# Moving the decay multiply of two batch groups in a clipped recurrence from VectorE to ScalarE

## The chip, the cores and the metric

The kernel runs on one core of a Trainium2 chip. A core has engines with queues of their own: PE (TensorE: matmuls and transposes, with weight loads as PEld), DVE (VectorE), ACT (ScalarE), POOL (GpSimd) and SP (SyncE, which here only issues DMAs). Each engine takes its own instructions in order, and they wait for each other through semaphores. The metric is the device time of one execution in microseconds; less is better.

## What is computed

Four layers run one after the other on x of 32 batches, 128 tokens and 512 channels: a recurrent layer, two attention layers, and a second recurrent layer. The change touches the two recurrent layers. Cut to what matters, the reference computes this in each of them:

```python
xr, gate = split(x @ W_in.T)            # 1024 channels each; xr: bias, convolution over 4 tokens, silu
xn = layernorm(xr)
Bm, Cm, dt = split(xn @ W_xproj.T, 3)   # 16 states each
Ad = 1.0 + tanh(dt @ W_dt.T + b_dt) * 0.01 * -tanh(A_log)
Bd = Bm * minimum(norm(xn), 1.0)
def step(h, inputs):                    # h: 16 states x 1024 channels for each batch
    ad, bd, xt, ct = inputs
    h = clip(h * ad[:, :, None] + bd[:, :, None] * xt[:, None, :], -10.0, 10.0)
    return h, einsum('bd,bdh->bh', ct, h)
_, ys = scan(step, h0, (Ad, Bd, xn, Cm))
out = x + (ys + D * xn) * silu(gate) @ W_out.T
```

So each token multiplies the state by a decay for each batch and state, adds an outer product, clips at 10, and reads the state out.

## The kernel before, in words

A recurrent layer has two phases, with a barrier between them. The first, `project_phase` (names `l0a`, `l3a`), does everything that doesn't depend on the state. The second, `recurrence_phase` (names `l0r`, `l3r`), is the one that is changed. It runs four engines in step, under an order that is written out by hand for each of them.

**The state.** 32 batches are 4 groups (`GJ`, index j) of 8. 8 batches with 16 states each fill the 128 partitions, so the state of one group is a tile of 128 x 1024 in f32. `g[:, t, j, :]` holds it for the last 4 tokens (`TS`, index t). 128 tokens are 32 blocks (`NBLK`, index k) of 4, so a block has 16 VectorE operations. They are numbered n = 4t + j here, and "op 10" is the one with t = 2 and j = 2. The two layers have 512 each.

**The scaled state.** The state is kept divided by the running product of its decays, `prod`. Then no step has to multiply by a decay: the input term is divided by `prod` ahead of time (`feed`), the coefficients that read the state out are multiplied by it, and the bounds of the clip become plus and minus 10 / `prod`, different for each partition and token. A setup on VectorE (lines 1165 to 1184) makes them; POOL copies those of one block into `cf` (`bounds`, line 925). One custom VectorE instruction does a step (line 1196): it adds the new term from PSUM to the state of the token before and clips the sum between two scalars of one value per partition, read from `cf`.

**TensorE, for each block.** Eight slots, s = 2t + p. Each begins with a `spread` (line 999): four matmuls that write the outer products of ops n and n + 1 (n = 2s) into two of three PSUM tiles `pv`, which are used in turn. Since a tile is free only when VectorE has read it, `spread` waits for the op n - 2 (semaphore `gup`). Behind the `spread` each slot has one piece of other work (`after`, line 1054), in this order: a run of 8 matmuls of the output projection (`mix` run 1 for block k - 2), `read_out` of token 3 of block k - 1, `mix` run 2 for k - 2, `read_out` of token 0, `turns` (transposes of the gated output of k - 1, in two halves), `read_out` of token 1, `mix` run 0 for k - 1, `read_out` of token 2. `mix` run 0 waits for both halves of `zh` (semaphore `z_hi`, line 1044).

**ScalarE, for each block** (body at line 1119): `keep_y` copies the read-out from PSUM, `keep_out` the projected output; `high(k, m)` copies half m of the transposed output to `zt` (which frees the PSUM bank for the other half) and then, rounded, to `zh`. In the first block it first makes the rounded part `woh` of the 8 output weight tiles (lines 1123 to 1125).

**POOL, for each block** (body at line 957): `bounds`, `weigh` (the weights of the next block's `spread`, from `crow`, which SP loads), `gating` of the last half block, `readers` (the coefficients of the next block's `read_out`), `residual`, `low` twice, `gating`. In the first block it waits for all eight `woh` tiles in between (lines 967 to 971), and makes the remainders `wol`.

**SP.** It loads the weight tiles through a buffer of two, `wst`: tile c waits for the remainder of tile c - 2. Only behind the eighth comes the load of `crow` for block 2.

**VectorE, for each op** (line 1186): it waits until its own earlier op is done (`gup`) and until its outer product is in PSUM (`bmm`). At the first op of a token it also waits until the old state of that place has been read out (`ymm`).

Of the kernel before, what the change touches and what calls it, by code (L numbers as in the profile page):

```python
# [6 lines left out]
ALU = mybir.AluOpType  # L7
ACT = mybir.ActivationFunctionType
# [6 lines left out]
KD, KI = DM // P, DI // P  # L15
# [5 lines left out]
CLIP = 10.0  # L21
GJ = 4
GB = B // GJ
TS = 4
# [3 lines left out]
PAIR = 2  # L28
ROOM = 2 * GB + 1
ROUND = 6  # L30
HEAD = 4


class Phase:
# [34 lines left out]
def at_least(eng, sem, value):  # L69

    if not (isinstance(value, int) and value <= 0):
        eng.wait_ge(sem, value)


def hold(eng):

    eng.nop(nofuse=True)
# [695 lines left out]
def recurrence_phase(nc, tag, x_in, x_out, w, cst, dram, proj, stat, wsum, wbias, coef, sent):  # L773

    with Phase(nc, tag) as ph:
        g = ph.sb("g", [P, TS, GJ, DI])
# [6 lines left out]
        cf = ph.sb("cf", [P, 2, 3, TS, GJ])  # L783
# [9 lines left out]
        wst = ph.sb("wst", [P, 2, DM])  # L793
        woh = ph.sb("woh", [P, KI, DM], F32R)
        wol = ph.sb("wol", [P, KI, DM], F32R)
        pv = [ph.ps(f"pv{k}", DI) for k in range(3)]
# [9 lines left out]
        zero = g[:, 1, 2, 0:S]  # L806
# [13 lines left out]
        z_mm, z_ev, z_hi, z_lo, o_mm, o_ev, res, w_hi, w_lo = (ph.sem(n) for n in (  # L820
            "z_mm", "z_ev", "z_hi", "z_lo", "o_mm", "o_ev", "res", "w_hi", "w_lo"))
        zeroed, last_sum, last_z, last_res = (ph.sem(n) for n in ("zeroed", "last_sum", "last_z", "last_res"))
        block = ph.block()
        n_pairs = NBLK // 2
        JW = TS * GB
# [82 lines left out]
        def _(pool):  # L908
# [5 lines left out]
            pool.memset(cd[:, :, :, :, :], 0.0).then_inc(zeroed, 1)  # L914
            pool.wait_ge(zeroed, 1)
            pool.wait_ge(same_ld, 32)
            pool.wait_ge(step, 8 + 3 + GJ + 1 + 3)

            def weigh(k, q, uses):
                pool.wait_ge(cr_ld[q], 32 * uses)  # L920
# [168 lines left out]
        def _(act):  # L1089
# [9 lines left out]
            act.wait_ge(feed_turned, 1)  # L1099
            act.activation(feed_h.rearrange("s j i -> s (j i)"), pf, ACT.Copy).then_inc(feed_high, 1)  # L1100

            def keep_y(k, m):
                act.wait_ge(ymm, TS * k + PAIR * (m + 1))
                at_least(act, z_mm, PAIR * (k - 1) + m + 1)
                act.activation(y[:, m, :], py[:, :], ACT.Copy).then_inc(yev, 1)  # L1105

            def high(k, m):
                act.wait_ge(z_mm, PAIR * k + m + 1)
                at_least(act, o_mm, k)
                act.activation(zt[:, :, m, :], pzo[:, :].rearrange("p (e i) -> p e i", i=TS * GB), ACT.Copy).then_inc(z_ev, 1)  # L1110
                act.wait_ge(z_ev, PAIR * k + m + 1)
                act.activation(zh[:, :, m, :], zt[:, :, m, :], ACT.Copy).then_inc(z_hi, 1)

            def keep_out(k):
                act.wait_ge(o_mm, k + 1)
                at_least(act, res, k)
                act.activation(mixed[:, :], pzo[:, :], ACT.Copy).then_inc(o_ev, 1)

            def body(i, first, last):
                for q in range(2):  # L1120
                    k = 2 * i + q
                    if first and q == 0:
                        for c in range(KI):
                            act.wait_ge(w_ld[c % 2], 16 * (c // 2 + 1))
                            act.activation(woh[:, c, :], wst[:, c % 2, :], ACT.Copy).then_inc(w_hi, 1)
                    if not (first and q == 0):
                        keep_y(k - 1, 1)
                    if not first:
                        keep_out(k - 2)
                    if not (first and q == 0):  # L1130
                        high(k - 1, 0)
                        high(k - 1, 1)
                    keep_y(k, 0)

            blocks(act, n_pairs, body)
            for m in range(PAIR):
# [8 lines left out]
        def _(dve):  # L1145
            count = [0]

            def chain(ins):

                count[0] += 1  # L1150
                ins.then_inc(step, 1)
                dve.wait_ge(step, count[0])
# [15 lines left out]
            chain(dve.tensor_scalar(acol[:, 1:2], acol[:, 0:1], -0.01, None, ALU.mult))  # L1168
            chain(dve.tensor_scalar(decay, decay, acol[:, 1:2], 1.0, ALU.mult, ALU.add))
            for j in range(GJ):  # L1170
                chain(dve.tensor_tensor_scan(prod[:, j, :], decay[:, j, :], zero, 1.0, ALU.mult, ALU.add))
            chain(dve.reciprocal(inv, prod))
            out = [coef[:, c, :, :].rearrange("p s j -> p j s") for c in range(3)]
            turn = [pt[c].rearrange("p (j s) -> p j s", j=GJ) for c in range(2)]
# [1 line left out]
            dve.tensor_tensor(feed, turn[0], inv, ALU.mult).then_inc(fed, 1)  # L1176
            chain(dve.tensor_tensor(out[2], turn[1], prod, ALU.mult))
            chain(dve.tensor_scalar(out[0], inv, CLIP, None, ALU.mult))
            dve.wait_ge(feed_high, 1)
            dve.tensor_tensor(feed_l.rearrange("s j i -> s (j i)"), pf, feed_h.bitcast(F32).rearrange("s j i -> s (j i)"),  # L1180
                              ALU.subtract).then_inc(feed_low, 1)
# [4 lines left out]
            def body(k):  # L1186
                dve.wait_ge(cfc, k.count(1, 1))
                for t in range(TS):
                    for j in range(GJ):
                        n = GJ * t + j  # L1190
                        if j == 0:
                            at_least(dve, ymm, k.count(TS, t - TS + 1))
                        dve.wait_ge(gup, k.count(GJ * TS, n + 1))
                        dve.wait_ge(bmm, k.count(GJ * TS, n + 1))
                        hold(dve)
                        dve._custom_dve(bass.dve_ops.TENSOR_ADD_SAT, out=g[:, t, j, :],  # L1196
                                        in0=g[:, (t - 1) % TS, j, :], in1=pv[(k.off + t + j) % 3][:, :],
                                        s0=cf[:, k.parity(), 0, t, j:j + 1], s1=cf[:, k.parity(), 1, t, j:j + 1]).then_inc(gup, 1)

            rounds(dve, body)  # L1200
            dve.wait_ge(ymm, TS * NBLK)
# [1112 lines left out]
```

## Time and profile before

| what | us |
|---|---|
| median of 3 runs (3762.84 to 3764.57) | 3763.84 |
| the profiled execution's own time | 3766.1 |
| its span, first to last instruction | 3764.3 |
| first VectorE step of layer 0 | 525.81 |
| first VectorE step of layer 3 | 3100.15 |
| VectorE busy with the steps, layer 0 and layer 3 | 641.9 and 641.8 |

The profiled execution is 2.3 us above the median, and 1.8 us of its time lie outside its span. The differences that are worked out below come from its trace and are put on the median. Over the whole span PE is busy 91%, DVE 79%, ACT 36% and POOL 50%; but these are averages over phases with different limits. The views that matter are the timeline of a recurrent block, the idle time ahead of the groups of the recurrence, and the timeline of the first two blocks.

### The profile page before, as it was taken

The page shows a single profiled execution, that of the slowest core. Times are in us where ns is not written, and L with a number is a line of the kernel's source. Part 1 is how long each engine was busy: PE and PEld are TensorE (multiplying, and loading weights), DVE is VectorE, ACT ScalarE, POOL GpSimd, SP SyncE. Part 2 cuts the span into 40 slices and gives each one's busy share as a digit, 9 for nine tenths or more (in the row PEclk, how much of TensorE's full clock was granted, in tenths as well). Part 3 has the DMA queues.
Part 4 walks back from the last instruction along what each step waited for, and adds up shares of the span by engine and source line. Part 5 has one row for each costly group of instructions (what it writes and reads, how often), then busy time and mean ns, then how long its engine had stood idle before and what let it go on. Part 6 is the DMA issues. An engine that isn't in the chain of part 4 may idle for free. (4 is left out here: it accounts for less than half of the span.)

```text
span 3764.3 us, 62060 instructions
## 1 busy us (share of the span) xinstructions
PE 3412.0 (91%) x22068; PEld 2260.9 (60%) x22068; DVE 2965.0 (79%) x3172; ACT 1355.2 (36%) x2078; POOL 1868.6 (50%) x1384
## 2 busy tenths in 40 slices
PE   7999839999996899999999999997999948999998
PEld 6777614444443667777777777775777733444444
DVE  4777769999996777777778777763576769999998
ACT  3555512221222553444444444432455522122121
POOL 2555645655563024444454444433355655556554
PEclk9999959999998899999999999998999968999999
DMA  4566765565554224222322222224466675555553
GB/s 128 217 259 257 271 239 203 203 219 214 200 215 142 80 72 138 85 82 78 111 96 87 80 83 85 74 63 133 162 259 237 257 294 196 217 201 210 216 206 136
DMA packets 288573, 631.00 MB, mean 168 GB/s; under 512 B 33472, under 2 KB 35904, under 8 KB 288224
## 3 DMA queue, kind: packets, MB, share of 16 engines
q1 hardware_dynamic: 281200, 615.49, 46.6%
q10 hardware_dynamic: 7104, 11.81, 0.9%
q8 instruction: 183, 3.00, 0.3%
q14 instruction: 86, 0.70, 0.1%
HBM read 390.75 MB, written 241.70 MB: 168 GB/s over the span
## 5 line engine op out<-in xcount | busy, mean ns | idle before, releaser
L1196 DVE CUSTOM_DVE_ANT_0 l0r_g<-l0r_g,l0r_pv,l0r_cf 128x1024 f32<-128x1024 f32 x512 | 641.9, 1336 | 20.6 <-PE l0r_pv L1005 19.0
L1196 DVE CUSTOM_DVE_ANT_0 l3r_g<-l3r_g,l3r_pv,l3r_cf 128x1024 f32<-128x1024 f32 x512 | 641.8, 1337 | 17.8 <-PE l3r_pv L1005 16.2
L137 PE MATMUL l1h_ps_p<-l1h_xh,l1c_wh 128*128 128x512 f32 x768 | 323.3, 421 | 5.6 <-issue 3.3
L139 PE MATMUL l1h_ps_p<-l1h_xl,l1c_wh 128*128 128x512 f32 x768 | 306.3, 399 | 0.0
L138 PE MATMUL l1h_ps_p<-l1h_xh,l1c_wl 128*128 128x512 f32 x768 | 304.9, 397 | 0.0
L2182 POOL TENSOR_TENSOR l1h_st<-l1h_veps 128x1 f32<-128x1 f32 x64 | 35.4, 554 | 530.5 <-DVE l1h_veps L2040 530.5
L1794 ACT ACTIVATE l1h_pt<-l1h_ps_t 128x512 f32<-128x512 f32 x256 | 151.4, 591 | 330.7 <-PE l1h_ps_t L1667 330.7
L1020 PE MATMUL l0r_py<-l0r_g,l0r_cd 128*32 128x512 f32 x2048 | 253.1, 613 | 1.3 <-ACT l0r_y L1105 1.3
L1020 PE MATMUL l3r_py<-l3r_g,l3r_cd 128*32 128x512 f32 x2048 | 252.0, 611 | 0.8 <-ACT l3r_y L1105 0.8
L2080 DVE TENSOR_TENSOR l1h_e<-l1h_e,l1h_mx 128x1024 f32<-128x1024 f32 x128 | 207.2, 1619 | 4.4
L2099 DVE TENSOR_TENSOR l1h_vt<-l1h_ps_p,l1c_dc 128x512 f32<-128x512 f32 x64 | 44.3, 691 | 194.6 <-PE l1h_ps_p L139 194.6
L1005 PE MATMUL l0r_pv<-l0r_x,l0r_wv 32*128 32x512 f32 x1024 | 132.3, 503 | 50.6 <-DVE l0r_g L1196 29.7
L1787 ACT ACTIVATE l1h_e<-l1h_e 128x1024 f32<-128x1024 f32 x128 | 134.9, 1054 | 118.8 <-DVE l1h_e L2023 117.5
L1005 PEld LDWEIGHTS l0r_pv<-l0r_x,l0r_wv 32*128 32x128 f32 x1024 | 53.5, 185 | 206.3 <-issue 137.0
L1005 PE MATMUL l3r_pv<-l3r_x,l3r_wv 32*128 32x512 f32 x1024 | 131.4, 499 | 50.5 <-DVE l3r_g L1196 29.4
L1005 PEld LDWEIGHTS l3r_pv<-l3r_x,l3r_wv 32*128 32x128 f32 x1024 | 53.2, 184 | 205.8 <-issue 136.8
L627 DVE SCALAR_TENSOR_TENSOR l3a_pacc<-l3a_pad,l3a_wconv,l3a_pacc 128x512 f32<-128x512 f32 x192 | 144.8, 754 | 34.6 <-ACT l3a_pacc L485 30.1
L627 DVE SCALAR_TENSOR_TENSOR l0a_pacc<-l0a_pad,l0a_wconv,l0a_pacc 128x512 f32<-128x512 f32 x192 | 144.8, 754 | 34.1 <-ACT l0a_pacc L485 29.5
L2207 POOL TENSOR_TENSOR l1h_vl<-l1h_vt,l1h_vh 128x512 fp32r<-128x512 f32 x64 | 123.7, 1933 | 92.2 <-ACT l1h_vh L1825 92.2
L1667 PE MATMUL l1h_ps_t<-l1h_ident,l1h_e 128*128 128x128 f32 x1024 | 161.8, 281 | 6.4 <-ACT l1h_pt L1794 5.6
L139 PEld LDWEIGHTS l1h_ps_p<-l1h_xl,l1c_wh 128*128 128x128 f32 x768 | 145.9, 190 | 36.2
L137 PEld LDWEIGHTS l1h_ps_p<-l1h_xh,l1c_wh 128*128 128x128 f32 x768 | 146.4, 191 | 33.6 <-issue 4.3
(400 smaller groups left out, 8965.1 us busy)
## 6 DMA issues: line engine op xcount, KB each, us to landing
l0r_x<-xhl_s SPq DMA_DIRECT2D x128, 512.0 KB, 5.9
l3r_x<-xhl_s SPq DMA_DIRECT2D x128, 512.0 KB, 5.7
xhl_s<-l0a_xo SPq DMA_DIRECT2D x116, 512.0 KB, 4.6
xhl_s<-l3a_xo SPq DMA_DIRECT2D x116, 512.0 KB, 4.6
gate_s<-l0a_gate SPq DMA_DIRECT2D x64, 256.0 KB, 3.0
l0r_dx<-dx_s SPq DMA_DIRECT2D x32, 512.0 KB, 7.7
l0r_gate<-gate_s SPq DMA_DIRECT2D x32, 512.0 KB, 8.6
l0r_crow<-feed_s SPq DMA_DIRECT2D x64, 256.0 KB
```

The costliest lines, as they stand in the source:

```text
L137: pe.matmul(out, wh, xh, start=first, stop=False)
L138: pe.matmul(out, wl, xh, start=False, stop=False)
L139: return pe.matmul(out, wh, xl, start=False, stop=last)
L627: dve.scalar_tensor_tensor(out=a, in0=pad[:, it % 2, :, c:c + S], scalar=wconv[:, it, c:c + 1], in1=a, op0=ALU.mult, op1=ALU.add).then_inc ...
L1005: last = pe.matmul(pv[(k.off + t + 2 * p + a) % 3][:, h * HALF:(h + 1) * HALF], wv[r, k.parity(), 2 * t + p, :], x[r, k.parity(), t, p, :] ...
L1020: last = pe.matmul(py[j * JW:(j + 1) * JW, :], cd[:, k.parity(), t, j, at:at + JW], g[:, t, j, h * HALF:(h + 1) * HALF], start=t % 2 == 0 ...
L1196: dve._custom_dve(bass.dve_ops.TENSOR_ADD_SAT, out=g[:, t, j, :], in0=g[:, (t - 1) % TS, j, :], in1=pv[(k.off + t + j) % 3][:, :], s0=cf[: ...
L1667: last = pe.transpose(ps_t[:, h * S:(h + 1) * S], e[:, k.mod(2), u // 2, h, u % 2, :], ident[:, :])
L1787: act.activation(e[:, k.mod(2), half, :, :, :], e[:, k.mod(2), half, :, :, :], ACT.Exp).then_inc(exp_ok, 1)
L1794: act.activation(pt[:, u % 2, :, :], ps_t[:, :].rearrange("p (h s) -> p h s", h=HG), ACT.Copy).then_inc(pt_ok, 1)
L2080: dve.tensor_tensor(block, block, total.unsqueeze(3).to_broadcast([P, HG, 2, S]), ALU.mult).then_inc(en_ok, 1)
L2207: pool.tensor_tensor(vl[:, n.mod(2), :, :], vt[:, n.parity(), :, b * S:(b + 1) * S], vh[:, n.mod(2), :, :].bitcast(F32), ALU.subtract).the ...
```

## The change

Groups j = 0 and j = 2 (`ACTED`) keep the state unscaled. For them `prod` is 1, `cf` holds the decay in place of the upper bound, and a step is two instructions: ScalarE multiplies the state of the token before by the decay (`age`), into the place of the new one, and VectorE adds the PSUM term to it and clips, with the constants 10 and -10 in place of two values per partition. Groups 1 and 3 stay as they are. A semaphore `aged` tells VectorE that the multiply is done.

ScalarE's list for a block is rewritten around the multiplies. The two copies of `high` are separate functions now, `keep_z` (to `zt`) and `high` (to `zh`). The eight weight copies of the first block are cut in two: four at the end of block 0, four in block 1. The code of TensorE and SP is not changed, nor is POOL's, but for the count of setup steps it waits for. `HEAD` wasn't used.

```diff
-HEAD = 4
+ACTED = (0, 2)
...
+            def high_weights(lo, hi):
+                for c in range(lo, hi):
+                    act.wait_ge(w_ld[c % 2], 16 * (c // 2 + 1))
+                    act.activation(woh[:, c, :], wst[:, c % 2, :], ACT.Copy).then_inc(w_hi, 1)
+
...
-            def high(k, m):
+            def keep_z(k, m):
                 act.wait_ge(z_mm, PAIR * k + m + 1)
                 at_least(act, o_mm, k)
                 act.activation(zt[:, :, m, :], pzo[:, :].rearrange("p (e i) -> p e i", i=TS * GB), ACT.Copy).then_inc(z_ev, 1)
+
+            def high(k, m):
                 act.wait_ge(z_ev, PAIR * k + m + 1)
                 act.activation(zh[:, :, m, :], zt[:, :, m, :], ACT.Copy).then_inc(z_hi, 1)
+
+            def age(k, q, t):
+                for j in ACTED:
+                    if t == j == 0:
+                        act.wait_ge(cfc, k + 1)
+                    if j == ACTED[0]:
+                        at_least(act, ymm, TS * (k - 1) + t + 1)
+                    act.wait_ge(gup, GJ * TS * k + GJ * t + j + 1)
+                    act.activation(g[:, t, j, :], g[:, (t - 1) % TS, j, :], ACT.Copy, scale=cf[:, q, 0, t, j:j + 1]).then_inc(aged, 1)
...
                     if first and q == 0:
-                        for c in range(KI):
-                            act.wait_ge(w_ld[c % 2], 16 * (c // 2 + 1))
-                            act.activation(woh[:, c, :], wst[:, c % 2, :], ACT.Copy).then_inc(w_hi, 1)
+                        age(0, 0, 0)
+                    age(k, q, 1)
+                    if first and q == 1:
+                        high_weights(KI // 2, KI)
                     if not (first and q == 0):
                         keep_y(k - 1, 1)
                     if not first:
                         keep_out(k - 2)
+                    age(k, q, 2)
                     if not (first and q == 0):
+                        keep_z(k - 1, 0)
                         high(k - 1, 0)
+                        keep_z(k - 1, 1)
+                    age(k, q, 3)
+                    if not (first and q == 0):
                         high(k - 1, 1)
                     keep_y(k, 0)
+                    if not (last and q == 1):
+                        age(k + 1, 1 - q, 0)
+                    if first and q == 0:
+                        high_weights(0, KI // 2)
...
             for j in range(GJ):
-                chain(dve.tensor_tensor_scan(prod[:, j, :], decay[:, j, :], zero, 1.0, ALU.mult, ALU.add))
+                if j in ACTED:
+                    chain(dve.memset(prod[:, j, :], 1.0))
+                else:
+                    chain(dve.tensor_tensor_scan(prod[:, j, :], decay[:, j, :], zero, 1.0, ALU.mult, ALU.add))
...
+            for j in ACTED:
+                chain(dve.tensor_copy(out[0][:, j, :], decay[:, j, :]))
...
+                        if j in ACTED:
+                            dve.wait_ge(aged, k.count(TS * len(ACTED), t * len(ACTED) + ACTED.index(j) + 1))
                         hold(dve)
-                        dve._custom_dve(bass.dve_ops.TENSOR_ADD_SAT, out=g[:, t, j, :],
-                                        in0=g[:, (t - 1) % TS, j, :], in1=pv[(k.off + t + j) % 3][:, :],
-                                        s0=cf[:, k.parity(), 0, t, j:j + 1], s1=cf[:, k.parity(), 1, t, j:j + 1]).then_inc(gup, 1)
+                        if j in ACTED:
+                            dve._custom_dve(bass.dve_ops.TENSOR_ADD_SAT, out=g[:, t, j, :], in0=g[:, t, j, :],
+                                            in1=pv[(k.off + t + j) % 3][:, :], s0=CLIP, s1=-CLIP).then_inc(gup, 1)
+                        else:
+                            dve._custom_dve(bass.dve_ops.TENSOR_ADD_SAT, out=g[:, t, j, :],
+                                            in0=g[:, (t - 1) % TS, j, :], in1=pv[(k.off + t + j) % 3][:, :],
+                                            s0=cf[:, k.parity(), 0, t, j:j + 1], s1=cf[:, k.parity(), 1, t, j:j + 1]).then_inc(gup, 1)
```

## Rows read from the trace of the kernel before

**Rows 1.** Page part 5, steps: shapes xcount | busy us, mean ns | idle before, releaser

```profile
L1196 DVE CUSTOM_DVE_ANT_0 l3r_g<-l3r_g,l3r_pv,l3r_cf 128x1024 f32<-128x1024 f32 x512 | 641.8, 1337 | 17.8 <-PE l3r_pv L1005 16.2
```

**Rows 2.** Timeline, layer 3, later blocks: start us, us, instruction xcount [idle before <-releaser]

```profile
3477.76 22.62 DVE L1196 CUSTOM_DVE_ANT_0 l3r_g<-l3r_g,l3r_pv,l3r_cf 128x1024 f32<-128x1024 f32 x18
...
3496.65 0.60 ACT L1110 ACTIVATE l3r_zt<-l3r_pzo 128x512 f32<-128x512 f32 x1 [2.92 <-PE l3r_pzo L1026]
3497.28 0.63 ACT L1112 ACTIVATE l3r_zh<-l3r_zt 128x512 fp32r<-128x512 f32 x1
...
3497.39 0.63 PE L1026 MATMUL l3r_pzo<-l3r_ident,l3r_y 128*128 128x128 f32 x4 [0.78 <-ACT l3r_zt L1110]
...
3500.53 0.51 PE L1005 MATMUL l3r_pv<-l3r_x,l3r_wv 32*128 32x512 f32 x4 [0.22 <-DVE l3r_g L1196]
3500.97 0.51 PE L1049 MATMUL l3r_pzo<-l3r_woh,l3r_zh 128*128 128x512 f32 x1
```

**Rows 3.** Windows, one block's length: busy us of PE, PEld, DVE, ACT, POOL; PEclk

```profile
3480.00:3500.00 20.00, 18.52 (x132) 8.58 (x128) 20.00 (x17) 4.25 (x7) 11.84 (x11) 1.00 0.57 209
```

**Rows 4.** Groups of VectorE by shape: none, and one, value per partition as scalar

```profile
L2023 DVE TENSOR_TENSOR l1h_e<-l1h_ps_s,l1h_mx 128x1024 f32<-128x1024 f32 x128 | 156.4, 1222 | 3.8 <-issue 0.3
L646 DVE SCALAR_TENSOR_TENSOR l3a_xn<-l3a_ptr,l3s_stat,l3a_grow 128x1024 f32<-128x1024 f32 x32 | 41.1, 1284 | 3.4 <-POOL l3a_stage L748 3.2 <-issue 0.2
```

**Rows 5.** Groups of ScalarE by shape: with and without a scale per partition

```profile
L510 ACT ACTIVATE l3a_xn<-l3a_xn,l3s_stat 128x1024 f32<-128x1024 f32 x28 | 32.1, 1146 | 0.0
L525 ACT ACTIVATE l3a_xo<-l3a_xn 128x1024 fp32r<-128x1024 f32 x30 | 31.5, 1051 | 4.3 <-DMA xhl_s<-l3a_xo 3.5 <-POOL l3a_xn L739 0.9
```

**Rows 6.** Timeline, end of layer 3: matmul runs, and one waiting for ScalarE

```profile
3745.78 0.51 PE L1049 MATMUL l3r_pzo<-l3r_woh,l3r_zh 128*128 128x512 f32 x1
...
3747.84 1.92 PE L1020 MATMUL l3r_py<-l3r_g,l3r_cd 128*32 128x512 f32 x16
...
3753.29 0.60 ACT L1139 ACTIVATE l3r_zh<-l3r_pv 128x512 fp32r<-128x512 f32 x1
...
3754.04 0.48 PE L1049 MATMUL l3r_pv<-l3r_woh,l3r_zh 128*128 128x512 f32 x1 [1.38 <-ACT l3r_zh L1139]
```

**Rows 7.** Timeline, first two blocks of layer 3, lines of five engines

```profile
3100.15 10.11 DVE L1196 CUSTOM_DVE_ANT_0 l3r_g<-l3r_g,l3r_pv,l3r_cf 128x1024 f32<-128x1024 f32 x8 [12.67 <-PE l3r_pv L1005]
...
3110.83 0.50 PE L1005 MATMUL l3r_pv<-l3r_x,l3r_wv 32*128 32x512 f32 x4
...
3111.47 5.10 DVE L1196 CUSTOM_DVE_ANT_0 l3r_g<-l3r_g,l3r_pv,l3r_cf 128x1024 f32<-128x1024 f32 x4 [1.20 <-issue]
...
3116.55 1.13 SPq L852 DMA_DIRECT2D l3r_crow<-feed_s  x2
...
3117.00 5.09 DVE L1196 CUSTOM_DVE_ANT_0 l3r_g<-l3r_g,l3r_pv,l3r_cf 128x1024 f32<-128x1024 f32 x4 [0.44 <-issue]
...
3118.75 0.63 ACT L1125 ACTIVATE l3r_woh<-l3r_wst 128x512 fp32r<-128x512 f32 x1 [0.78 <-DMA l3r_wst<-L_W_outT]
3119.28 0.58 ACT L1105 ACTIVATE l3r_y<-l3r_py 128x512 f32<-128x512 f32 x1
...
3128.96 2.35 POOL L922 TENSOR_TENSOR l3r_wv<-l3r_crow,l3r_same 128x1024 fp32r<-128x1024 f32 x1 [5.12 <-DMA l3r_crow<-feed_s]
3131.26 1.28 POOL L943 TENSOR_TENSOR l3r_y<-l3r_y,l3r_dx 128x512 f32<-128x512 f32 x1
...
3135.70 30.15 DVE L1196 CUSTOM_DVE_ANT_0 l3r_g<-l3r_g,l3r_pv,l3r_cf 128x1024 f32<-128x1024 f32 x24 [0.96 <-PE l3r_pv L1005]
```

**Rows 8.** DMA issues of that stretch: xcount, KB each, median us to landing

```profile
l3r_wst<-L_W_outT SPq DMA_DIRECT2D x8, 256.0 KB, 2.7
```

**Rows 9.** Attention: a longer idle time of PE, and the windows row behind it

```profile
1582.52 0.47 PE L137 MATMUL l1h_ps_p<-l1c_wh,l1h_vh 128*128 128x512 f32 x1 [1.67 <-issue]
...
1583.00:1592.00 9.00, 9.00 (x57) 7.02 (x57) 6.79 (x10) 4.89 (x7) 2.85 (x4) 1.00 0.16 53
```

**Rows 10.** Setup of layer 3: the scans that make the running product

```profile
L1171 DVE TENSOR_TENSOR_SCAN l3r_g<-l3r_g 128x128 f32<-128x128 f32 x4 | 1.7, 424 | 0.1
```

More of the change, by code:

```diff
@@ L822, in recurrence_phase @@
         zeroed, last_sum, last_z, last_res = (ph.sem(n) for n in ("zeroed", "last_sum", "last_z", "last_res"))
+        aged = ph.sem("aged")
         block = ph.block()
@@ L916, in _ @@
             pool.wait_ge(same_ld, 32)
-            pool.wait_ge(step, 8 + 3 + GJ + 1 + 3)
+            pool.wait_ge(step, 8 + 3 + GJ + 1 + 3 + len(ACTED))
             def weigh(k, q, uses):
```

## The prediction

> **What bounds the kernel now.** I read four views. The page's costliest groups come first: the custom step has 512 instructions in each recurrent layer, 641.8 us busy and only 17.8 us idle ahead of them in layer 3 [rows 1]. So VectorE sets the pace there. The timeline of later blocks gives that pace: 18 steps fill 22.62 us and the last of them takes 1.34, so one starts every (22.62 - 1.34) / 17 = 1.252 us, and a block of 16 takes 20.03 us [rows 1, 2]. A step overlaps the one before by 0.08 us. The windows view of one block shows who is next: PE 18.52 us busy out of 20.00, ACT 4.25, POOL 11.84 [rows 3]. PE is close behind, and in the timeline it waits for VectorE 0.22 us ahead of a `spread` [rows 2]. Last, the timeline of the first two blocks shows the one stretch where VectorE waits for others: gaps ahead of the steps at 3111.47, 3117.00 and 3135.70 [rows 7]. So a gain must come from a faster VectorE, and it lasts only while PE, close behind and waiting for ScalarE twice in a block, can follow.
>
> **The change part by part.**
>
> *The step with constant bounds.* It isn't in the trace. The step with two values per partition as scalars takes 1.337 us [rows 1]. A two-input VectorE instruction of the same shape, one input from PSUM as well, takes 1.284 with one such scalar and 1.222 with none [rows 4]. So I take 1.222, a start every 1.222 - 0.084 = 1.138 us. The bounds are 1.337 (constants cost the same) and, as an estimate, 1.14, if a scalar cost this instruction 0.1 us and not 0.06. VectorE alone would then need 8 x 1.252 + 8 x 1.138 = 19.12 us for a block: 0.91 less than now, 57 us over 62 blocks (all but the first in each layer).
>
> *The multiply on ScalarE.* The nearest row has the same form, 128 x 1024 in f32 with a scale per partition: 1.146 us. Without the scale it is 1.051 [rows 5]. Bounds 1.05 and 1.25. Eight of them add 9.2 us to ScalarE's 4.25 for each block [rows 3], so it has room. The multiply for an op can start when the op of the same group one token earlier is done, and three ops lie between: 3.5 us, enough for 1.15. So VectorE's new wait for `aged` hides behind its own work, as long as ScalarE gets to the multiply in time.
>
> The Trainium skill ("ScalarE: Activation LUTs", Rules for kernel authors) says to put a multiplication on VectorE and not on ScalarE. By that rule alone the exchange is bad, 1.15 us of ScalarE for 0.11 us of VectorE, and if nothing hid it, it would add (1.146 - 0.114) x 512 = 528 us; ScalarE's 15.75 us of idle time in a block [rows 3] say that it is hidden, so the rule doesn't settle the case.
>
> *What is queued behind the multiplies.* This decides. ScalarE's new order puts `age(k, 3)`, the multiplies for ops 12 and 14, ahead of the second `high(k - 1, 1)`. The multiply for op 14 waits for op 10. So the second half of `zh` can't be made before op 10 ends and its multiply is through. PE's `mix` run 0 in the seventh slot waits for that half, and PE's queue holds the `spread` of ops 14 and 15 behind it. Now that half is ready long before: the two pairs of `zt` and `zh` copies follow right behind the transposes, and the run starts 0.44 us behind its `spread` [rows 2].
>
> Counted from the start of op 10: op 10 takes 1.22; ScalarE starts 0.03 later (as `zh` behind `zt` [rows 2]); the multiply takes 1.15; the `zh` copy takes 0.63, but overlaps the instruction in front by 0.10 when it isn't waiting, as `keep_y` at 3119.28 does with the copy at 3118.75 [rows 7], so 0.53; PE's first matmul comes 0.15 after a `zh` copy ends (3753.89 to 3754.04), and a run of 8 holds the next work of another shape back for 3747.84 - 3745.78 = 2.06 [rows 6]; from a `spread` to the op that waits for it 3111.47 - 3110.83 = 0.64 [rows 7]. Sum 5.78 us. Op 14 would otherwise start 4 ops behind op 10, after 4.78. It comes 1.00 us late in every block.
>
> *One block.* The loop that closes runs from op 14 of one block to op 10 of the next, 12 starts (6 x 1.252 + 6 x 1.138 = 14.34), and then along that path: 14.34 + 5.78 = 20.12 us, against 20.03 now. The 0.91 that VectorE saves is spent at the `mix` run. This waits in blocks 2 to 31, 30 per layer: 60 x 0.09 = +5 us. Its bounds: with the multiply at 1.05, or without the overlap of 0.10, a block moves by 0.1 us; with 1.19 or 1.26 for the step (seven of them lie on the loop) by 0.2 to 0.3. So 19.9 to 20.45, or -8 to +25 us.
>
> *The first two blocks.* The eight `woh` copies now start at the first step; they move to the end of block 0 (four) and into block 1 (four). Three queues are behind them. POOL waits in its list for all eight before `readers(1)`, both `gating` of block 0 and `weigh(2)`. SP loads `crow` for block 2 only behind the eighth tile. And ScalarE stands in the second four while multiplies wait. In layer 3, counted from the first step (3100.15):
>
> - Op 14 of block 0 starts at 3117.00 + 2 x 1.2, so 19.2, perhaps 0.4 sooner with faster steps. It ends at 20.0, and its successor's multiply at 21.2; here the copies begin.
> - A tile costs a copy of 0.63, a POOL subtraction of 1.28 (other POOL work of that shape takes as long [rows 7]), and a load of 2.7 [rows 8] before the tile two further on can be copied: some 4.7 us for two tiles. Tiles 2 and 3 are copied by 27.8. The two multiplies of `age(1, 1)` come in between, until 30.1. POOL is done with tile 5 at about 34.0, and SP goes on to `crow` at 34.5.
> - Now `crow` for block 2 is issued at 3116.55 and `weigh` starts at 3128.96, which waited for it: 12.4 us [rows 7]. So `weigh(2)` runs from 46.9 to 49.3, and the last `gating` of block 0 (two instructions of 1.28) until 51.9.
> - PE's second half of `turns` in block 1 waits for that (0.13 and 0.56), then the `spread` (0.64): op 10 of block 1 starts at about 53. Before, it is the third of the run that starts at 3135.70: 3138.2, so 38.1.
>
> That is 15 us later in layer 3. With the copies, the loads or `crow` somewhat sooner it is 10; with PE at the lower clock after such a wait it is 17. I take 14 in each of the two layers: +28 us, bounds 20 and 34.
>
> *The setup.* Two of four scans of 0.42 us each [rows 10] become memsets and two small copies are added. Gain or loss is under 1 us in each layer, taken as 0.
>
> *At no cost:* `HEAD`, the two semaphore waits that are satisfied early (`ymm` in `age`, `cfc`), `keep_y` and `keep_out` behind multiplies (they come about 1 us later; their readers, `gating` and `turns`, have that much: if not, it is the seventh slot's kind of loss, and lies in the bounds).
>
> **The sum.** 3763.84 + 5 + 28 = 3797 us. From the bounds, 3763.84 - 8 + 20 = 3776 to 3763.84 + 25 + 34 = 3823.
>
> **The rivals.**
>
> - *The constants save nothing* (the change doesn't do what it says): the step stays 1.337. For it: the step is a custom instruction, and none of its kind with constants is in the trace. Against: the rows with no, one and two such scalars rise by about 0.06 each [rows 1, 4]. Then the loop is 12 x 1.252 + 5.78 + 0.11 = 20.91, 60 x 0.88 = +53, with 28 for the first blocks 3845 us. The Trainium skill ("VectorE: DVE Perf Modes", the errata section's table) prices a VectorE instruction with PSUM source by its length alone, without a term for the scalar's kind; by that table this rival holds, and the three rows speak against it.
> - *PE isn't late* (faster): op 14 gets its `spread` in time because the path behind op 10 is 1.0 us shorter than my 5.78, so that VectorE's 19.12 holds. It decides at 4.78. For it: every piece is a row of another place. Against: the multiply, the copy and the run of 8 alone are 3.74 and can't overlap. 3763.84 - 0.91 x 60 + 28 - 2 = 3735 us; halfway, at 5.3, still 3765.
> - *The first blocks are hidden* (no change): `crow` and the weights land sooner, or later blocks give the time back. For it: the loads share the queue with less than now. Against: steady blocks have no slack to give back. 3763.84 + 5 = 3769 us, a little less with faster steps.
> - *The lower PE clock.* While it waits 1.2 us more in each block, PE could be granted 0.5 and not 1.00 for a stretch. Each matmul of the run then starts 0.2 us later, 1.6 us for a block: 60 x 1.6 more, 3893 us. Against: behind an idle time of 1.67 us the windows row reads 1.00 [rows 9], and with 0.78 in each block it reads 1.00 now [rows 2, 3].
>
> **How the numbers follow.** Chances: the forecast 0.68, no saving 0.09, PE not late 0.10, first blocks hidden 0.08, lower clock 0.05. The range 3762 to 3850 takes in nearly all of the forecast, the hidden first blocks and most of the case without a saving; it leaves out the fast case and the lower clock and little more: 0.8. About 0.2%, 7.5 us, is what a measurement of this kernel can tell from no change. Faster by more than that: the fast case and the low end of the others, 0.11. Within it: the hidden case and a little of the forecast, 0.09. Slower: 0.80.
>
> **What would show it.** In the profile after: steps with constants at 1.22 us; ScalarE's multiply at 1.15; PE idle about 1.2 us ahead of `mix` run 0, released by ScalarE's `zh`, in every later block; VectorE idle about 1 us ahead of op 14, released by the `spread`; a block still 20.1 us; and op 10 of block 1 some 14 us later than before. The prediction is wrong if blocks are at 19.1 to 19.5 us, or if block 1 shows no long wait for the weights.

## The result, and the profile after

| | before | after |
|---|---|---|
| median, us | 3763.34 (3762.48 to 3764.57) | 3805.18 (3803.95 to 3806.64) |
| after over before, 95% interval | | 1.0107 (1.0091 to 1.0122) |
| span of the profiled execution | 3764.3 | 3803.0 |
| op 10 of block 1, from the layer's first step: layer 0, layer 3 | 40.8, 38.1 | 53.2, 54.3 |
| first step of block 2, likewise | 48.4, 45.6 | 62.2, 62.5 |
| a later block (the median) | 20.04 | 20.16 |

The change makes the kernel 1.1% slower. The forecast was 3797 with a range from 3762 to 3850. The medians differ by 41.8 us, the two profiled spans by 38.7. The rest is scatter: the profiled execution of before lay 2.8 us above the median of this table, that of after 0.35 below its own. All places below are worked out from the spans.

The title is not exact: before, no engine multiplied by the decay in a step, since the bounds and coefficients took it in through `prod`. For groups 0 and 2 the multiply on ScalarE is new work, and what VectorE drops is the reading of two bounds per partition.

First the groups of the recurrence in the page of after (shapes xcount | busy us, mean ns | idle before, releaser), which answer to [rows 1] and [rows 5]:

```profile
L1129 ACT ACTIVATE l3r_g<-l3r_g,l3r_cf 128x1024 f32<-128x1024 f32 x256 | 293.7, 1149 | 195.0 <-DVE l3r_g L1231 188.7
...
L1231 DVE CUSTOM_DVE_ANT_0 l3r_g<-l3r_g,l3r_pv 128x1024 f32<-128x1024 f32 x256 | 311.5, 1217 | 64.2 <-issue 36.7
...
L1234 DVE CUSTOM_DVE_ANT_0 l3r_g<-l3r_g,l3r_pv,l3r_cf 128x1024 f32<-128x1024 f32 x256 | 342.0, 1336 | 0.0
```

The step with constants is there and takes 1.217 us, the multiply 1.149. VectorE's steps are (1336 - 1217) x 256 ns = 30.5 us shorter in each layer, and its idle time ahead of them has risen from 17.8 [rows 1] to 64.2 us. Of these 46 us more, 26.4 lie ahead of op 14 in the 30 later blocks and 18.5 in the first two. The timeline of one later block of layer 3 shows the first part (start, duration, engine, line, what; in brackets the idle time and its releaser; rows that this reading doesn't need are left out):

```profile
3480.08 1.22 DVE L1231 CUSTOM_DVE_ANT_0 l3r_g<-l3r_g,l3r_pv 128x1024 f32<-128x1024 f32 x1 [0.89 <-issue]
...
3494.50 1.22 DVE L1231 CUSTOM_DVE_ANT_0 l3r_g<-l3r_g,l3r_pv 128x1024 f32<-128x1024 f32 x1
3495.75 1.15 ACT L1129 ACTIVATE l3r_g<-l3r_g,l3r_cf 128x1024 f32<-128x1024 f32 x1 [0.25 <-DVE l3r_g L1231]
...
3496.81 0.61 ACT L1120 ACTIVATE l3r_zh<-l3r_zt 128x512 fp32r<-128x512 f32 x1
3497.57 0.48 PE L1050 MATMUL l3r_pzo<-l3r_woh,l3r_zh 128*128 128x512 f32 x1 [1.01 <-ACT l3r_zh L1120]
...
3499.61 0.50 PE L1006 MATMUL l3r_pv<-l3r_x,l3r_wv 32*128 32x512 f32 x4
...
3500.24 1.22 DVE L1231 CUSTOM_DVE_ANT_0 l3r_g<-l3r_g,l3r_pv 128x1024 f32<-128x1024 f32 x1 [0.89 <-issue]
```

The rows are op 14 of the block before, op 10, the multiply for op 14, the second `zh` copy, the first matmul of `mix` run 0, the `spread` of ops 14 and 15, and op 14. From op 10 on, each begins within 0.15 us of the end of the one above it (for the `spread`, of the run that the row above opens). In before the run began 0.44 us behind its `spread`, without a wait [rows 2]; now PE stands 1.01 us idle there, and VectorE 0.89 ahead of op 14. The windows view of after (window, length, then busy us and count of PE, PEld, DVE, ACT and POOL, the granted clock, DMA share and GB/s), of the stretch that [rows 3] show of before:

```profile
3480.00:3500.00 20.00, 18.21 (x128) 8.37 (x126) 19.25 (x16) 12.89 (x15) 11.82 (x10) 1.00 0.57 210
```

ScalarE goes from 4.25 to 12.89 us and is still idle a third of the time: it isn't short of time; it comes too late to one instruction. PE holds its granted clock of 1.00 (2.4 GHz).

Last, the timeline of the first two blocks of layer 3 in after, which answers to [rows 7]:

```profile
3116.93 1.22 DVE L1231 CUSTOM_DVE_ANT_0 l3r_g<-l3r_g,l3r_pv 128x1024 f32<-128x1024 f32 x1 [12.47 <-PE l3r_pv L1006]
...
3139.39 1.13 ACT L1106 ACTIVATE l3r_woh<-l3r_wst 128x512 fp32r<-128x512 f32 x2
...
3152.31 1.13 SPq L853 DMA_DIRECT2D l3r_crow<-feed_s  x2
...
3154.71 0.63 ACT L1106 ACTIVATE l3r_woh<-l3r_wst 128x512 fp32r<-128x512 f32 x1 [0.92 <-DMA l3r_wst<-L_W_outT]
...
3164.28 2.34 POOL L923 TENSOR_TENSOR l3r_wv<-l3r_crow,l3r_same 128x1024 fp32r<-128x1024 f32 x1 [4.48 <-DMA l3r_crow<-feed_s]
...
3169.23 1.12 PE L1027 MATMUL l3r_pzo<-l3r_ident,l3r_y 128*128 128x128 f32 x4 [6.67 <-POOL l3r_y L947]
...
3171.20 1.22 DVE L1231 CUSTOM_DVE_ANT_0 l3r_g<-l3r_g,l3r_pv 128x1024 f32<-128x1024 f32 x1 [6.98 <-issue]
```

The weight copies begin 22.5 us after the first step and end at 38.4; SP issues `crow` at 35.4, `weigh` starts at 47.4 when it has landed, the half `turns` waits for POOL until 52.3, and op 10 of block 1 starts at 54.3.

**Where the 38.7 us come from.** The first two blocks: 13.8 us in layer 0 and 16.9 in layer 3, together 30.7. The 30 later blocks of each layer: 5.1 and 4.5, together 9.5 (before rounding). What lies ahead of the first step of layer 0: -0.2; between the last step of layer 0 and the first of layer 3 (the attention layers and the second setup): -1.9. Behind the last step: +0.6 (17.2 to 17.8 us until the end).

### The profile page after: what moved, and what is told of

The parts are those of the page before. It is cut to its first block and busy times, and to the rows that moved or that the text cites. A ratio compares the mean times of both kernels' runs of the same rounds, so it can differ in the third digit from the quotient of the medians.

```text
span 3803.0 us, 63540 instructions
## 1 busy us (share of the span) xinstructions
PE 3403.6 (89%) x22068; PEld 2255.7 (59%) x22068; DVE 2916.7 (77%) x3176; ACT 1907.3 (50%) x2590; POOL 1857.9 (49%) x1384
## 5 line engine op out<-in xcount | busy, mean ns | idle before, releaser
L1129 ACT ACTIVATE l0r_g<-l0r_g,l0r_cf 128x1024 f32<-128x1024 f32 x256 | 293.7, 1148 | 195.4 <-DVE l0r_g L1231 189.2
L1129 ACT ACTIVATE l3r_g<-l3r_g,l3r_cf 128x1024 f32<-128x1024 f32 x256 | 293.7, 1149 | 195.0 <-DVE l3r_g L1231 188.7
L1231 DVE CUSTOM_DVE_ANT_0 l3r_g<-l3r_g,l3r_pv 128x1024 f32<-128x1024 f32 x256 | 311.5, 1217 | 64.2 <-issue 36.7
L1231 DVE CUSTOM_DVE_ANT_0 l0r_g<-l0r_g,l0r_pv 128x1024 f32<-128x1024 f32 x256 | 311.5, 1217 | 64.0 <-issue 36.2
L1234 DVE CUSTOM_DVE_ANT_0 l3r_g<-l3r_g,l3r_pv,l3r_cf 128x1024 f32<-128x1024 f32 x256 | 342.0, 1336 | 0.0
L1234 DVE CUSTOM_DVE_ANT_0 l0r_g<-l0r_g,l0r_pv,l0r_cf 128x1024 f32<-128x1024 f32 x256 | 342.0, 1336 | 0.0
L2220 POOL TENSOR_TENSOR l1h_st<-l1h_veps 128x1 f32<-128x1 f32 x64 | 35.4, 552 | 531.7 <-DVE l1h_veps L2078 531.7
```

What stands on the lines that cost most here:

```text
L1129: act.activation(g[:, t, j, :], g[:, (t - 1) % TS, j, :], ACT.Copy, scale=cf[:, q, 0, t, j:j + 1]).then_inc(aged, 1)
```

## The experiments

Each kernel is the changed one with one edit, with three exceptions: the third has the first two edits, the seventh has these and one more, and the fourth is the kernel before with one edit. The ratio is to the kernel before, measured on the same chip beside it (its medians there: 3768.06 for the first four, 3769.48 for the others), with its 95% interval. The theory of the prediction is called the first. "Op 10 of block 1" is always counted from the layer's first step.

**1. The second `zh` copy ahead of the multiplies.** This takes away the waiting of op 14 and leaves the first blocks alone.

```diff
+                        high(k - 1, 1)
                     age(k, q, 3)
-                    if not (first and q == 0):
-                        high(k - 1, 1)
                     keep_y(k, 0)
```

> The changed kernel with one line moved: ScalarE makes the second zh copy (high(k-1,1)) ahead of the multiplies for ops 12 and 14, not behind them. Theory 1 (the mix run that waits for this copy costs the 1.0 us in each block): VectorE's own pace is left, 19.1 to 19.2 us for a block in place of 20.16, and no idle time ahead of op 14. 60 blocks x 1.0 = 60 us less than the changed kernel: about 3745 us, below the kernel before. Rival (PE has no room, 18.5 us busy in 20, so that a block can't be shorter than some 19.7 whatever waits go): 3775 to 3800 us, with PE busy throughout and VectorE waiting for the spread in other slots. The first two blocks stay as late as in the changed kernel in both.

Measured: 3743.92 us (3735.05 to 3744.70), ratio 0.9932 (0.9916 to 0.9949). Most blocks take 19.07 to 19.09 us; op 10 of block 1 at 52.9 and 52.6. The timeline of a later block of this kernel (columns as above):

```profile
3469.32 0.64 ACT L1120 ACTIVATE l3r_zh<-l3r_zt 128x512 fp32r<-128x512 f32 x1
...
3469.45 1.22 DVE L1230 CUSTOM_DVE_ANT_0 l3r_g<-l3r_g,l3r_pv 128x1024 f32<-128x1024 f32 x1
...
3469.86 2.18 ACT L1129 ACTIVATE l3r_g<-l3r_g,l3r_cf 128x1024 f32<-128x1024 f32 x2
...
3471.31 0.50 PE L1050 MATMUL l3r_pzo<-l3r_woh,l3r_zh 128*128 128x512 f32 x1
...
3474.22 1.22 DVE L1230 CUSTOM_DVE_ANT_0 l3r_g<-l3r_g,l3r_pv 128x1024 f32<-128x1024 f32 x1
```

Now `zh` starts before op 10 does (3469.45), the run begins 0.44 us behind its `spread` (at 3470.87) again, without a wait, and op 14 follows op 10 after 4.77 us: its place in the pace. The place of one ScalarE instruction of 0.6 us in its list is worth 1.08 us for each block (20.16 against 19.07 to 19.09).

**2. The weight copies spread over block 0**, two behind each token's multiplies. This is the other half alone: the waiting of op 14 stays.

```diff
                     age(k, q, 1)
-                    if first and q == 1:
-                        high_weights(KI // 2, KI)
+                    if first and q == 0:
+                        high_weights(0, 2)
...
                     age(k, q, 2)
...
+                    if first and q == 0:
+                        high_weights(2, 4)
...
+                    if first and q == 0:
+                        high_weights(4, 6)
                     keep_y(k, 0)
...
                     if first and q == 0:
-                        high_weights(0, KI // 2)
+                        high_weights(6, KI)
```

> The changed kernel with the eight weight copies of ScalarE spread over block 0, two behind each token's multiplies, none in block 1. Theory 1 (the late copies hold POOL, SP and with them block 1 back): op 10 of block 1 comes at about 38 us after the first step, as in the kernel before, and not at 53 to 54; block 2 begins some 15 us sooner in each layer; later blocks stay at 20.16. About 30 us less: 3775 us. Rival (the delay in block 1 has another source, the lower PE clock or the multiplies themselves): under 10 us less, 3795 us or more.

Measured: 3778.08 us (3777.14 to 3779.78), ratio 1.0028 (1.0016 to 1.0041). Blocks of 20.16 us as in after; op 10 of block 1 at 39.0 and 38.2. The timeline of the first two blocks of layer 3:

```profile
3105.36 1.22 DVE L1235 CUSTOM_DVE_ANT_0 l3r_g<-l3r_g,l3r_pv 128x1024 f32<-128x1024 f32 x1 [12.66 <-PE l3r_pv L1006]
...
3124.68 1.13 SPq L853 DMA_DIRECT2D l3r_crow<-feed_s  x2
...
3136.59 2.37 POOL L923 TENSOR_TENSOR l3r_wv<-l3r_crow,l3r_same 128x1024 fp32r<-128x1024 f32 x1 [3.73 <-DMA l3r_crow<-feed_s]
...
3143.55 1.22 DVE L1235 CUSTOM_DVE_ANT_0 l3r_g<-l3r_g,l3r_pv 128x1024 f32<-128x1024 f32 x1 [3.34 <-issue]
```

`crow` is issued at 19.3 instead of 35.4, and everything behind it is as much sooner: op 10 of block 1 is where it was before the change. The kernel is still 10 us slower than before, which is about what the later blocks lost by themselves (9.5).

**3. Both edits together.**

> Both moves together: the second zh copy ahead of the multiplies, and the weight copies spread over block 0. Theory 1 (two separate losses, 60 us in the later blocks and 30 us in the first two): they add up, 3805 - 90 = 3715 us, with 19.1 to 19.2 us for a block. Rival (PE takes over as the bound once VectorE is faster): blocks at 19.4 us or more, 3735 us or more.

Measured: 3712.89 us (3708.77 to 3718.70), ratio 0.9854 (0.9837 to 0.9870). Blocks of 19.07 to 19.10 us, op 10 of block 1 at 38.9 and 39.2. The windows view of a later stretch (columns as above):

```profile
3480.00:3500.00 20.00, 18.81 (x132) 8.89 (x132) 19.79 (x18) 13.76 (x17) 11.95 (x10) 1.00 0.63 222
```

VectorE is busy 19.79 of 20 us again. This version is faster than both kernels: 55 us below before, where the change as made is 42 above it.

**4. The constants alone, in the kernel before**, without the multiply.

```diff
+                        bound = (CLIP, -CLIP) if j in (0, 2) else [cf[:, k.parity(), c, t, j:j + 1] for c in range(2)]
                         dve._custom_dve(bass.dve_ops.TENSOR_ADD_SAT, ...
-                                        s0=cf[:, k.parity(), 0, t, j:j + 1], s1=cf[:, k.parity(), 1, t, j:j + 1]).then_inc(gup, 1)
+                                        s0=bound[0], s1=bound[1]).then_inc(gup, 1)
```

> The kernel before, with nothing changed but the bounds of groups 0 and 2, which are the constants 10 and -10: no multiply on ScalarE, and its order as before. It leaves out that the bounds of these groups should follow the running product of the decays. It prices the VectorE saving alone. Theory 1: steps of 1.217 us, starts every 1.13, a block 19.1 us, 62 x 0.94 = 58 us less than the kernel before: 3705 us. Rival (PE, close behind, takes most of the gain): 19.5 us or more for a block, 3730 us or more.

Measured: 3710.61 us (3705.03 to 3711.56), ratio 0.9847 (0.9830 to 0.9863), blocks of 19.07 us. So this is what the constants are worth where nothing else is changed, 57 us, and the third experiment reaches it within 2.3 us, less than either one's scatter: 512 multiplies of 1.149 us, 588 us of ScalarE's time, cost nothing that can be measured here.

**5. The bounds 10 and -10 read from a tile**, one value per partition, in place of the constants.

```diff
+            for c in range(2):
+                chain(dve.memset(ten[:, c:c + 1], CLIP * (1 - 2 * c)))
...
-                                            in1=pv[(k.off + t + j) % 3][:, :], s0=CLIP, s1=-CLIP).then_inc(gup, 1)
+                                            in1=pv[(k.off + t + j) % 3][:, :], s0=ten[:, 0:1], s1=ten[:, 1:2]).then_inc(gup, 1)
```

> The changed kernel, but the bounds 10 and -10 of groups 0 and 2 are read from a tile with one value per partition, so that their steps take as long as the others (1.336). All waits and orders as in the changed kernel. Theory 1 (a block is the loop of twelve VectorE starts and the path through the multiply, the zh copy and the mix run): 12 x 1.252 + 5.9 + 0.1 = 21.0 us for a block, 60 x 0.85 = 51 us more than the changed kernel, about 3856 us, though VectorE alone would need only 20.04. Rival (a block of the changed kernel is held by PE's own work, and VectorE's step time doesn't matter as long as it stays under that): at most 10 us more, 3815 us or less.

Measured: 3855.37 us (3850.00 to 3860.22), ratio 1.0228 (1.0206 to 1.0250). The timeline, op 14 of two blocks in a row and the `mix` run ahead of the second:

```profile
3498.85 1.34 DVE L1234 CUSTOM_DVE_ANT_0 l3r_g<-l3r_g,l3r_pv,l3r_ten 128x1024 f32<-128x1024 f32 x1 [0.75 <-issue]
...
3517.07 0.47 PE L1051 MATMUL l3r_pzo<-l3r_woh,l3r_zh 128*128 128x512 f32 x1 [1.19 <-ACT l3r_zh L1121]
...
3519.73 1.34 DVE L1234 CUSTOM_DVE_ANT_0 l3r_g<-l3r_g,l3r_pv,l3r_ten 128x1024 f32<-128x1024 f32 x1 [0.75 <-issue]
```

The same numbers as bounds, read from a tile, cost 0.12 us a step (1.336). A block takes 20.88 to 20.89 us, though 16 steps by themselves would need 20.03. So the length of VectorE's steps and the late copy add up: the loop runs through both. This is the first rival of the prediction, made real; it priced such a block at 20.91.

**6. The load of `crow` for block 2 ahead of the weight tiles** in SP's list.

```diff
+                        load_feed(2, 0)
...
-                            load_feed(k + 1, 1 - q)
+                            if not (first and q == 1):
+                                load_feed(k + 1, 1 - q)
```

> The changed kernel with SP's load of crow for block 2 issued ahead of the eight weight tiles, not behind the last. Theory 1 (weigh(2) on POOL waits for this load, and the last gating of block 0 and PE's transposes stand behind it): op 10 of block 1 comes 4 to 6 us sooner, at 48 to 50 us after the first step; 8 to 12 us less in two layers, about 3795 us. Rival (POOL's wait for the eight weight tiles alone sets it): under 2 us less, 3803 us or more.

Measured: 3795.24 us (3793.89 to 3800.03), ratio 1.0071 (1.0051 to 1.0091); blocks of 20.16 us; op 10 of block 1 at 49.1 and 47.7. The timeline of layer 3: the issue, the last two remainders on POOL, the last `gating` of block 0, and op 10:

```profile
3102.04 11.81 SPq L853 DMA_DIRECT2D l3r_crow<-feed_s  x6
...
3148.83 2.65 POOL L973 TENSOR_TENSOR l3r_wol<-l3r_wst,l3r_woh 128x512 fp32r<-128x512 f32 x2 [1.99 <-ACT l3r_woh L1108]
...
3158.21 1.26 POOL L949 TENSOR_TENSOR l3r_y<-l3r_y,l3r_gate 128x512 f32<-128x512 f32 x1
...
3161.49 1.22 DVE L1233 CUSTOM_DVE_ANT_0 l3r_g<-l3r_g,l3r_pv 128x1024 f32<-128x1024 f32 x1 [2.98 <-issue]
```

With the six issues of `crow` in one go before the first step, POOL's wait for `crow` is gone, and op 10 comes 4.1 and 6.6 us sooner than in after; of the 12.4 and 16.2 us that it had lost in layers 0 and 3, 8.3 and 9.6 stay. So `crow` behind the tiles is one part of that loss, and the smaller one. The rest goes with the copies themselves (experiment 2 undoes it), through POOL, which waits in its list for all eight of them: here it waits 1.99 us for `woh` ahead of the last two remainders, then works without a wait until that `gating` ends at 3159.47, and op 10 follows 2.0 us behind.

**7. Three groups on ScalarE**, on top of the third experiment.

```diff
-ACTED = (0, 2)
+ACTED = (0, 1, 2)
```

> The version with both moves (second zh copy first, weight copies spread over block 0), and three groups instead of two with the multiply on ScalarE and constant bounds. VectorE alone would need 12 x 1.131 + 4 x 1.252 = 18.58 us for a block in place of 19.07, ScalarE 12 x 1.15 + 4.25 = 18 us. Theory 1 (PE is just behind: its slots with 0.43 for a spread and 1.86 to 2.06 for the rest add to some 18.9 us, and ScalarE, full now, comes late with some copies): no more than 12 us less than with two groups, 3700 to 3730 us, with VectorE waiting for the spread. Rival (VectorE is still the bound): 62 x 0.49 = 30 us less, 3683 us.

Measured: 3729.21 us (3725.29 to 3731.84), ratio 0.9890 (0.9871 to 0.9910), blocks of 19.38 us: slower than with two groups, though VectorE has 4 x 0.12 us less to do in a block. A window, and the timeline around one half of `turns`:

```profile
3400.00:3420.00 20.00, 18.93 (x140) 8.59 (x132) 19.62 (x18) 17.32 (x21) 12.41 (x12) 1.00 0.59 214
```

```profile
3428.36 3.22 ACT L1129 ACTIVATE l3r_g<-l3r_g,l3r_cf 128x1024 f32<-128x1024 f32 x3
...
3431.48 0.58 ACT L1116 ACTIVATE l3r_zt<-l3r_pzo 128x512 f32<-128x512 f32 x1
...
3432.20 0.63 PE L1027 MATMUL l3r_pzo<-l3r_ident,l3r_y 128*128 128x128 f32 x4 [1.06 <-ACT l3r_zt L1116]
...
3433.39 1.22 DVE L1234 CUSTOM_DVE_ANT_0 l3r_g<-l3r_g,l3r_pv 128x1024 f32<-128x1024 f32 x1 [0.27 <-issue]
```

This looks like the same mechanism at another piece of PE's work: three multiplies stand ahead of `zt`, and the second half of `turns` waits 1.06 us for it, where it waited 0.78 before the change [rows 2] and in experiment 3. The 0.28 more is most of the 0.31 by which a block is longer than in experiment 3, and VectorE's longest idle time in a block, 0.27, is ahead of op 10, right behind that. No run moves this copy, so that its place costs the time is not shown.

**8. One more ScalarE copy of 0.61 us ahead of the late `zh`**, from block 2 on, on top of after.

```diff
+                    if not first:
+                        act.activation(wst[:, 1, :], wst[:, 0, :], ACT.Copy)
                     if not (first and q == 0):
                         high(k - 1, 1)
```

> The changed kernel with one more ScalarE copy of 128 x 512 (from one half of the weight buffer, which isn't used any more, into the other) between the multiply for op 14 and the second zh copy, from block 2 on. It writes nothing that the result needs. ScalarE has the room: 13.4 us busy in 20.16. Theory 1 (each microsecond between op 10 and the mix run lengthens a block): 0.53 to 0.63 us more for a block, 60 x 0.58 = 35 us more than the changed kernel, 3840 us. Rival (the copy is late but not what ends last): under 10 us more, 3815 us or less.

Measured: 3843.65 us (3843.52 to 3848.22), ratio 1.0201 (1.0181 to 1.0220). Most blocks take 20.66 us, 0.50 more than in after: what is put into that path (0.61, less the 0.10 by which a copy overlaps the one before it) is paid in every block. A few take more; the timeline of PE in one of them, and in the block before it:

```profile
3464.23 0.48 PE L1050 MATMUL l3r_pzo<-l3r_woh,l3r_zh 128*128 128x512 f32 x1 [1.53 <-ACT l3r_zh L1120]
...
3466.26 0.50 PE L1006 MATMUL l3r_pv<-l3r_x,l3r_wv 32*128 32x512 f32 x4
...
3485.16 0.48 PE L1050 MATMUL l3r_pzo<-l3r_woh,l3r_zh 128*128 128x512 f32 x1 [1.71 <-ACT l3r_zh L1120]
...
3487.82 0.63 PE L1050 MATMUL l3r_pzo<-l3r_wol,l3r_zh 128*128 128x512 f32 x1
3488.38 0.80 PE L1006 MATMUL l3r_pv<-l3r_x,l3r_wv 32*128 32x512 f32 x4
```

and the window behind that second wait:

```profile
3485.70:3489.10 3.40, 3.40 (x11) 1.95 (x9) 0.73 (x1) 0.84 (x1) 3.20 (x3) 0.50 0.12 48
```

The granted clock is 0.50 (1.2 GHz) there, and the run takes 3.2 us instead of 2.03. This is the last rival of the prediction; it needed a longer wait than the change brings (see the end).

## Why the prediction was right

The forecast was 33 us more than before; the spans give 38.7. The two large terms were each too small (5 for 9.5, 28 for 30.7), and 1.5 us came off elsewhere.

**The place and the mechanism held.** The prediction said that the gain of VectorE is spent at `mix` run 0, because the second `zh` copy stands behind a multiply that waits for op 10. Experiment 1 moves that copy alone and gets blocks of 19.07 us; the sum of the prediction for VectorE by itself was 19.12. Experiments 5 and 8 lengthen the loop in two other places and pay for both.

**The terms of the path.** Op 10 to its multiply: 1.25 forecast and measured. The multiply until the copy starts: 1.06 (forecast 1.15, with the overlap counted at the copy). The copy until PE's first matmul: 0.76 (0.53 + 0.15; together with the multiply 1.82 against 1.83). The run until the next `spread`: 2.04 (2.06). From there to op 14: 0.63 (0.64). Together 5.74 against 5.78. Op 14 came 0.97 us late, forecast 1.00. The wait that the prediction named for PE, 1.2 us, reads 1.01.

**The step with constants**: 1.217 against 1.222. By the Trainium skill ("VectorE: DVE Perf Modes", the errata section's table), in which the scalar's kind has no price, the step would have stayed as it was. Experiment 5 settles it: one instruction, one shape, the same values, 1.336 from a tile and 1.217 as constants.

**The multiply on ScalarE.** The rule of the Trainium skill ("ScalarE: Activation LUTs", Rules for kernel authors) that keeps multiplications on VectorE doesn't decide this case: experiments 3 and 4 differ by 2.3 us for 512 multiplies. What costs is where they stand in ScalarE's list, not that they are there.

**The later blocks: mechanism right, size off.** The term was 60 x 0.09 = 5 us; it is 9.5. The loop itself was 14.42 us from op 14 to op 10 where the prediction had 14.34, since op 0, the first step behind ops 14 and 15, loses its overlap: it starts 1.36 us after op 15, 0.11 more than the pace, 0.02 behind the end of op 15's record and not 0.08 ahead of it. In experiment 1, where op 14 isn't late, this doesn't happen. But a late op 14 alone doesn't explain it: in experiment 5 op 14 waits 0.75 us and op 0 keeps its 1.25, and in experiment 7 op 14 waits under 0.05 and op 0 takes 1.36. What takes the overlap is open (the `spread` for op 0 starts 0.84 us ahead of it, so PE isn't far off). The 58 pitches between the `mix` runs of the later blocks are 9.5 us longer together. Ten long ones, told of below, make 2.8 of this; 6.7 are left, 0.115 for each pitch and not 0.09. The 2.8 are single pauses of VectorE. This timeline of VectorE shows one:

```profile
3445.53 1.34 DVE L1234 CUSTOM_DVE_ANT_0 l3r_g<-l3r_g,l3r_pv,l3r_cf 128x1024 f32<-128x1024 f32 x1
3447.05 1.22 DVE L1231 CUSTOM_DVE_ANT_0 l3r_g<-l3r_g,l3r_pv 128x1024 f32<-128x1024 f32 x1 [0.18 <-DVE l3r_g L1234]
```

The second step starts 1.52 us after the first, 0.27 late. Such pauses stand behind steps 43, 93, 143, 243, 343 and 443 of layer 3 (counted from 0). Of the 58 pitches six in layer 0 and four in layer 3 are longer than the others, by 0.23 to 0.34 us, 2.8 us together; steps 43 and 443 are op 11 of their blocks, beside the loop, and for step 443 the pitch stays at 20.16. The pauses stand behind the same steps in experiments 1, 2, 3, 6 and 8, and in experiment 4, where VectorE's list is nearly that of before, pauses of 0.26 to 0.34 us stand behind steps 67, 181 and 295 of layer 3, 114 apart. The even distance speaks for something periodic in VectorE's own stream; the cause stays open.

**The first two blocks**: 28 forecast, 30.7 measured, by the steps that were named. In layer 3 the copies began at 22.5 (21.2 forecast), `crow` was issued at 35.4 (34.5), `weigh` ran from 47.4 (46.9), the gating ended at 52.2 (51.9), op 10 started at 54.3 (53). The copies started 1.3 us late, and the waits behind them took up some of it. Between the gating and op 10 the prediction's terms (0.13 + 0.56 + 0.64) make 1.3 us, and it was 2.0: there the granted clock is 0.50 (3167.0 to 3171.2), the `spread` takes 0.80 us and half the `turns` 1.12. This is the case with PE at the lower clock, which had been priced at 17 us; layer 3 lost 16.9 and layer 0 13.8.

**The setup** gained 1.9 us or less where 0 was taken; the stretch also holds the attention layers, so the two are not told apart.

**The rivals.** The constants do save (experiment 5 is what it would be if not, 3855 against its 3845, on a before that read 6 us higher). PE is late (experiment 1 shows the opposite case, 3744, with the first blocks as in after). The first blocks aren't hidden (experiment 2 shows them undone: 3778 on a before of 3768). The lower clock did not appear in the later blocks of after. (The second rival's value at 5.3 us, 3765, comes out at 3766 by its own terms; nothing hangs on it.)

## What to carry to other kernels

When work is moved to an engine that has time to spare, go through that engine's list and ask of each instruction behind the new ones who waits for it: an instruction of 0.6 us that had been done long ahead became the last link of a loop, and undoing that one place turned 1.1% slower into 0.7% faster. A gain that a slower loop swallows can be seen in advance by adding up the chain from the instruction that the new wait needs to the one that the pace needs, and comparing it with the pace: 5.78 against 4.78 us here. And look at the first rounds by themselves, where one-off work sits in the same lists: of 39 us, 31 came from two blocks out of 32 in each layer.

## What the runs showed of the hardware

Two scalars of one value per partition cost the custom step 0.12 us: 1.336 us with them, 1.217 with two constants. No run has one of each; half of it would be 0.06, as between the rows with one and with none [rows 4].

The granted clock of PE fell from 1.00 to 0.50 in experiment 8, behind some waits and not behind others. Its later blocks have 50 waits of 1.52 to 1.55 us ahead of `mix` run 0, and the clock fell behind none of them; they have 10 of 1.71 or 1.72 (where a pause of VectorE falls on the loop), and it fell behind 5 of these, in the one shown 0.5 us after the matmuls had begun again. Such a block takes 22.15 to 22.18 us, 1.5 more than its neighbours. In after the longest wait there is 1.20 us, and no block is that long; before the change one idle time of 1.67 us passed at 1.00 [rows 9]. So a path that has grown by a few tenths of a microsecond can bring a second, larger loss now and then, and one wait that passed without it is no proof that the next of its length will.
